# A two-layer mixture-of-experts kernel: expert weights split during layer 0, their halves kept in DRAM, and GpSimd's routed work given to VectorE

## What is computed

```
x = x + ffn0(cond0(x))      # cond: a 64x64 matrix per sequence, gathered by index
x = x + ffn1(cond1(x))      # cond1 adds a bias column as well (the "side" input)

ffn0: one 512->2048->512 network with gelu, run twice per token (top 2 of 8 routes),
      each time with the low-rank additions of its route; weighted sum of both
ffn1: shared expert 512->704->512 over all tokens
      + routed experts: top 2 of 8, each silu(x Wg) * (x Wu) -> Wd, 512->352->512
```

## Time and profile before

| | us |
|---|---|
| runs shown | 1054.9, 1051.52 and 2602.53; median 1054.9 |
| the profiled execution | 1050.06 |
| its span, first to last instruction | 1048.2 |
| PE busy in the span | 1010.6 |
| DVE, ACT, POOL busy | 524.3, 314.4, 354.5 |
| TensorE's granted clock, mean | 0.993 of full |

### The profile page before, as it was taken

How to read it: one execution, slowest core, us unless ns; L and a number is a source line. 1 busy time by engine, 2 the same in 40 slices (tenths; PEclk the granted TensorE clock), 3 DMA queues, 4 the chain that set the end, 5 groups by cost and what they waited for, 6 DMA issues and landing times.

```text
span 1048.2 us, 14852 instructions
## 1 busy us (share of the span) xinstructions
PE 1010.6 (96%) x4893; PEld 837.2 (80%) x4895; DVE 524.3 (50%) x886; ACT 314.4 (30%) x550; POOL 354.5 (34%) x351
## 2 busy tenths in 40 slices
PE   8899999999999999999999999999989999999993
PEld 5678887888888887888867777778778999999992
DVE  3788777455565455555566333665543314443000
ACT  3743332211121112111242010301144545454541
POOL 4123245410000000000042000022168889898873
PEclk9999999999999999999999999999999999999997
DMA  7387543443433434453444101005155665665433
GB/s 239 130 297 272 161 136 122 166 161 114 140 123 121 153 128 161 142 181 123 138 159 151 41 1 41 1 1 198 58 187 108 163 163 142 141 146 119 80 61 40
DMA packets 51322, 136.41 MB, mean 130 GB/s; under 512 B 8708, under 2 KB 10004, under 8 KB 50772
## 3 DMA queue, kind: packets, MB, share of 16 engines
q1 hardware_dynamic: 36660, 108.15, 30.1%
q0 software_dynamic: 12432, 25.71, 12.4%
q10 hardware_dynamic: 2192, 2.08, 0.7%
HBM read 96.85 MB, written 39.07 MB: 130 GB/s over the span
## 4 chain that ended last, share of the span: by engine, by line
PE 85%; DVE 4%; POOL 4%; DMA 2%; issue 1%; ACT 1%; ACTq 1%; PEldq 0%; POOLq 0%; PEld 0%; DVEq 0%
PE ps_y L1687 6%; PE ps_y L1689 6%; PE ps_y L1688 5%; PE ps_h L1645 5%; PE ps_h L1647 5%; PE ps_h L1646 5%; PE ps_u L1700 3%; PE ps_u L1699 3%; PE ps_h L1933 2%; PE ps_y L1933 2%; PE ps_y L1928 2%; PE ps_y L1929 2%; PE ps_y L1856 2%; PE ps_y L1857 2%; PE ps_h L1840 2%; PE ps_h L1841 2%
## 5 line engine op out<-in xcount | busy, mean ns | idle before, releaser
L1202 DVE TENSOR_TENSOR h<-h,wb 128x512 f32<-128x512 f32 x64 | 44.4, 693 | 162.6 <-ACT h L903 162.5
L897 ACT ACTIVATE h<-ps_h,bias 128x512 f32<-128x512 f32 x64 | 44.0, 689 | 235.1 <-PE ps_h L1654 235.1
L685 POOL DMA_DIRECT2D s_raw<-in_sgu x8 | 4.3, 544 | 299.9 <-DVE g_lo L1210 192.1
L1687 PE MATMUL ps_y<-w_hi,g_hi 128*128 (+1 forms) x256 | 102.2, 399 | 3.5 <-DVE g_lo L1210 3.5
L1689 PE MATMUL ps_y<-w_hi,g_lo 128*128 (+1 forms) x256 | 101.2, 395 | 0.0
L1688 PE MATMUL ps_y<-w_lo,g_hi 128*128 (+1 forms) x256 | 101.0, 395 | 0.0
L1645 PE MATMUL ps_h<-xt_hi,w_hl 128*128 128x512 f32 x256 | 100.0, 391 | 0.7 <-ACT lg_t L846 0.7
L1647 PE MATMUL ps_h<-xt_hi,w_hl 128*128 128x512 f32 x256 | 100.3, 392 | 0.0
L1646 PE MATMUL ps_h<-xt_lo,w_hl 128*128 128x512 f32 x256 | 100.2, 391 | 0.0
L1477 DVE CAST eg_hi<-e_raw 128x704 fp32r<-128x704 f32 x32 | 16.7, 581 | 138.0 <-PE ps_y L1958 125.3
L903 ACT ACTIVATE h<-ps_h,bias 128x512 f32<-128x512 f32 x64 | 43.9, 688 | 115.4 <-PE ps_h L1667 115.4
(11 more groups left out here) (319 smaller groups left out, 2455.5 us busy)
## 6 DMA issues: line engine op xcount, KB each, us to landing
w_hl<-w1s_d SPq DMA_DIRECT2D x49, 704.0 KB, 4.1
w1s_d<-w_hl SPq DMA_DIRECT2D x16, 704.0 KB, 5.9
e_raw<-in_wgu SPq DMA_DIRECT2D x8, 1408.0 KB, 7.1
w_raw<-in_w1b SPq DMA_DIRECT2D x16, 608.0 KB, 4.7
xres<-in_x SPq DMA_DIRECT2D x16, 256.0 KB, 4.5
acc<-x_d SPq DMA_DIRECT2D x4, 1024.0 KB, 7.6
xc_d<-xc SPq DMA_DIRECT2D x4, 1024.0 KB, 4.8
e_raw<-in_wdn SPq DMA_DIRECT2D x8, 512.0 KB, 8.4
```

What stands on the lines that cost most here:

```text
L1202: tt(h1[u][:], h1[u][:], wb[:, v, :], ALU.mult).then_inc(gch, 1)
L1687: mm(ps_y[:, j, :], g_hi[u][:, cols], sl(w2_hi), start=first, **kw)
```

## The change

1. **Units in layer 0.** The weights of experts 1 to 7 come in a new input `we1`, 6 units of 128 x 768 for each, 42 units `k`. In layer 0, step 16 + k, for k from 0 to 41: GpSimd loads the unit to `pre_raw` (two buffers), ScalarE copies it to `pre_hi` (`high_unit`), VectorE subtracts in place (`low_unit`), and GpSimd stores both halves in DRAM, `e_d`. The load of unit k+1 is issued behind the two stores of unit k.
2. **The routed part loads halves.** `split_expert` stays for expert 0 alone. For experts 1 to 7 SyncE loads the four parts of the two halves from `e_d` (4.46 MB an expert), for expert 1 when the last shared gate/up product is done, for the others when the last tile of the expert two before is done.
3. **GpSimd's elementwise work goes to VectorE**, which reads PSUM directly; ScalarE's three copies `xg_f`, `ru`, `rgt_f` are dropped. GpSimd is left with gathers and scatters: `gather(t + 5)`, `scatter_add(t)`, where it was `scatter_add(t - 1)` behind the elementwise work.
4. **First tile earlier.** Gathers 0 and 1 go out when the slot lists are ready; `turn_x(0)` stands behind the first of the last four shared down products.
5. The bias column is packed into `cond1`; its 32 own loads are dropped, and the other 32 go into stage 0's loop over `low_w1`.

The core of the diff:

```diff
+            pool.wait_ge(w1_lo_done, 2 + FT)
+            pool.wait_ge(w2_lo_done, FT)
+            pool.wait_ge(z_ok, 4)
+            def load_unit(k):
+                u = k % 2
+                if k >= 2:
+                    pool.wait_ge(pre_st[u], 32 * (k // 2))
+                at = k % UNITS * UW
+                pool.dma_start(pre_raw[u], we1[k // UNITS, :, at:at + UW]).then_inc(pre_in[u], 16)
+            def store_unit(k):
+                u = k % 2
+                pool.wait_ge(pre_lo_done, k + 1)
+                at = k % UNITS * UW
+                for n, src in enumerate((pre_hi[u].bitcast(F32), pre_raw[u])):
+                    pool.dma_start(e_d[k // UNITS, n, :, at:at + UW], src).then_inc(pre_st[u], 16)
+            load_unit(0)
+            load_unit(1)
+            for k in range(AHEAD):
+                store_unit(k)
+                if 1 <= k < AHEAD - 1:
+                    load_unit(k + 1)
...
             for t in range(SLOT_TILES):
-                g_low(t)
-                if t + 1 < SLOT_TILES:
-                    products(t + 1)
-                if t + 2 < SLOT_TILES:
-                    x_low(t + 2)
                 if t + 5 < SLOT_TILES:
                     gather(t + 5)
-                if t:
-                    scatter_add(t - 1)
-            scatter_add(SLOT_TILES - 1)
+                scatter_add(t)
...
+            def high_unit(k):
+                act.wait_ge(pre_in[k % 2], 16 * (k // 2 + 1))
+                nc.scalar.copy(pre_hi[k % 2], pre_raw[k % 2]).then_inc(pre_hi_done, 1)
...
                     gelus(s * FT + f, f, f % 2, s - 1 if f == 1 else None)
+                    if (s - 1) * FT + f < AHEAD:
+                        high_unit((s - 1) * FT + f)
                     if s + 1 < NS and f == 1:
                         masks(s + 1)
...
+            def low_unit(k, u):
+                dve.wait_ge(pre_hi_done, k + 1)
+                tt(pre_raw[u].bitcast(F32R), pre_raw[u], pre_hi[u].bitcast(F32), ALU.subtract).then_inc(pre_lo_done, 1)
...
                     hidden_tile(s * FT, v, 0, sums=s - 1)
+                    low_unit((s - 1) * FT, 0)
                     add_moved(s - 1)
                     hidden_tile(s * FT + 1, v, 1)
+                    low_unit((s - 1) * FT + 1, 1)
...
+            def load_halves(e):
+                b, gu = e % 2, DC * 2 * H1
+                for k, (eg, ed) in enumerate(((eg_hi, ed_hi), (eg_lo, ed_lo))):
+                    sp.dma_start(eg[:, b].rearrange("p c n -> p (c n)").bitcast(F32),
+                                 e_d[e - 1, k, :, 0:gu]).then_inc(half_in, 16)
+                    sp.dma_start(ed[:, b].rearrange("p c n -> p (c n)").bitcast(F32),
+                                 e_d[e - 1, k, :, gu:gu + HC * D]).then_inc(half_in, 16)
...
+                    if (s, j) == (NS - 1, 0):
+                        turn_x(0, 0, 16, first=True)
```

More of the change, by code:

```diff
@@ L96, in adaln_ffn @@
                              for u in range(2)])
+        ahead = ExitStack()
+        sb_ahead = tensors(ahead)
+        pre_hi = [sb_ahead(f"pre_hi{u}", [P, UW], F32R)[:] for u in range(2)]
+        pre_raw = [sb_ahead("pre_raw0", [P, UW])[:], u1t[:, 0:UW]]
+        ahead.close()
         w_raw = [sb(f"w_raw{u}", [P, WROW]) for u in range(2)]
@@ L339, in adaln_ffn @@
         out_st = sem("out_st")
+        pre_in = [sem(f"pre_in{u}") for u in range(2)]
+        pre_hi_done = sem("pre_hi_done")
+        pre_lo_done = sem("pre_lo_done")
+        pre_st = [sem(f"pre_st{u}") for u in range(2)]
+        half_in = sem("half_in")
         e_in = sem("e_in")
@@ L953, in _ @@
             for h in range(2):
[L954 removed]
+                act.wait_ge(cw1_in[h], 16 * J)
             take_x(2)
@@ L997, in _, with x_high @@
                         rows_step(*rows_step_after_down(s, j))
-            def x_high(t, first=False):
+            def x_high(t):
                 act.wait_ge(xgt_done, t + 1)
                 nc.scalar.copy(xg_hi[:].rearrange("p c n -> p (c n)"), ps_u[:, 0, :]).then_inc(xg_hi_done, 1)
-                if not first:
-                    act.wait_ge(xg_lo_done, t)
-                nc.scalar.copy(xg_f[:], ps_u[:, 0, :]).then_inc(xg_f_done, 1)
             def silu(t, u, first=False):
@@ L1036, in copies @@
                     silu(t + 1, 1 - u)
-                g_high(t, first=stored is None and n == 0)
-                if nxt:
-                    up(t + 1, 1 - u)
+                g_high(t)
                 if nxt2:
@@ L1231, in low_s @@
                     dve.wait_ge(z_done, 2 + STEPS)
+                else:
+                    for u in range(2):
+                        dve.wait_ge(pre_st[u], 32 * (AHEAD // 2))
                 hi, lo, raw = shared_halves(n)
@@ L1869, in slot_sums, with turn_x @@
                 last.then_inc(oh_mm, 1)
+            def turn_x(t, u, n, first=False):
+                pe.wait_ge(xg_in[u], n)
+                if not first:
+                    pe.wait_ge(xg_lo_done, t)
+                for c in range(DC):
+                    last = nc.tensor.transpose(ps_u[:, 0, c * P:(c + 1) * P], xg[u][:, c * P:(c + 1) * P], ident[:])
+                last.then_inc(xgt_done, 1)
             cond_rows(2)
@@ L1906, in experts @@
                 return [(packed // E ** n % E, packed // E ** n % 2) for n in range(WINDOW)]
-            def turn_x(t, u, n, first=False):
-                pe.wait_ge(xg_in[u], n)
-                if not first:
-                    pe.wait_ge(xg_f_done, t)
-                for c in range(DC):
-                    last = nc.tensor.transpose(ps_u[:, 0, c * P:(c + 1) * P], xg[u][:, c * P:(c + 1) * P], ident[:])
-                last.then_inc(xgt_done, 1)
             def gate_or_up(t, u, eb, k):
@@ L1973, in _ @@
             pe.wait_ge(rg_zero, 1)
-            turn_x(0, 0, 16, first=True)
             e = experts(0)
```

149 lines of the change are left out of this document (77 added, 72 removed).

## The result

| | before | after |
|---|---|---|
| median | 1053.8 us | 1071.4 us |
| lowest to highest | 1051.5 to 1054.9, and one of 2602.5 | 1068.0 to 1074.1 |
| ratio after to before | | 1.017, 95% interval 1.013 to 1.022 |
| span of the profiled execution | 1048.2 | 1068.0 |
| TensorE's granted clock, mean | 0.993 | 0.983 |

What follows compares the result with a forecast made beforehand. TensorE was taken as the bound, busy 1010.6 of 1048.2 us. 1050.06 less 15.2 routed gains, plus 11.3 at stage starts and 9.9 steady growth, gave 1056.1; own range 1046 to 1073, 8-in-10 range 1036 to 1084.

Steps and rivals of the forecast that it cites:

- The stall at stage 2: Start of stage 2, layer 0: TensorE waits 8.3 us for a mask copy queued behind `high_unit(17)`, plus 1.7 for the clock.
- G: Layer 0: landing time of a unit's load, counted from the first store's issue; 4.8 to 5.4 us, taken as 4.8.
- the ring: Layer 0: a unit's cycle of copy, subtraction, issue and transfers, 2.2 + G = 7.0 us, just under the 7.39 step.
- The steady growth: Stages 1 and 3: overlap with `w_hl` adds between nothing and 1.9 us to G; half taken, 18 steps of 0.55, 9.9.
- The 1.0 for `gelu_first(50)`: Start of stage 3: `high_unit(33)` holds `gelu_first(50)` on ScalarE, so `second` comes 1.0 us late.
- (c): Routed part's tail: with `scatter_add(t)` the last scatter starts 2.2 us behind the last `yt` instead of 6.8, winning 4.6.
- (a): Routed part's head: 1.5 us won before the first gate, and 3.7 between `turn_g(0)` and `turn_g(1)`.
- (b): Routed part, tiles 1 to 37: 248.0 us falls to 36 tiles of 6.74, winning 5.4.
- A: Layer 0: the units are hidden after all, load 17 in time and the ring holding; 1036 us, chance 0.13.
- B: Layer 0: the ring outlasts the step in every stage, deciding at G above 5.2; 1115 us, chance 0.12.
- C: Routed part: its gain is given back by late scatters or a tile waiting for halves; 1066 us, chance 0.10.
- D: Layer 0: VectorE holds GpSimd's issues, 0.7 us in each of 33 steps; 1079 us, chance 0.06.

Runs made afterwards that it cites:

- the kernels with 254.0: Kernels where `turn_g(0)` to `turn_g(38)` took 254.0 us, among them the changed kernel with layer 0's units left out: median 1035.5 us, ratio 0.985.
- the last kernel with the units moved: Changed kernel with load before stores, no unit in the first two steps of stages 2 and 3, `s_raw` loads not between last units: 1044.7 us, ratio 0.992.
- masks first: Changed kernel with `masks(s+1)` ahead of `high_unit` on ScalarE at a stage's second step: median 1062.4 us, ratio 1.011.
- the pieces: Changed kernel with SyncE's 1 MB transfers in layer 0 each split in four of 256 KB, one a step: median 1062.9 us, ratio 1.012.

## Why the prediction was right, and where it was not

**The stall at stage 2: right.** Predicted: 8.3 us in L1699 behind load 17, and 1.7 for the clock. Measured: 8.04 us in the same instruction, by the same chain of three lists; `hidden(34)` is 10.7 late, so the rest is 2.7. The spell at 0.50 of the clock was 6.8 us long, not 3.4. That 8.04 is so near to 8.3 has luck in it: the load landed 0.5 us later behind the first store than I put it, and `low_unit(16)` ended 0.6 us sooner against the time at which L1750 was due (308.24 against 307.17, where I had 301.1 against 299.4).

**G: the wrong end taken.** Of 4.8 and 5.4 I took 4.8, since the first transfer is a store. It was 5.3 to 5.4 (5.3 above), the value that two loads of the trace gave. So the ring was 7.5 us instead of 7.0 and a little above a step from the start: the units of stage 1 were stored 7.56 us apart (204.74 to 250.09, six of them). TensorE lost little by it: outside the gaps the steps grew by 1.4 us in all in stage 1 and 1.2 in stage 2.

**The steady growth: wrong, and with it the sum.** I put 9.9 us as 18 steps of 0.55, from the overlap with `w_hl`. Steps 0.55 longer hardly exist. In their place came four gaps, 20 us together, that no term of mine holds. The step that failed is the one that looked at one step of the trace and took `w_hl` as all that SyncE sends. At the second step of a stage it also sends 1 MB, in stage 3 another two times 1 MB. And the bound "all of 1.9" for a meeting was too low, as the run with a quarter of the bytes shows: there a load took 4.3 us more than by the median. One gap of the four, 6.1 us at `hidden(56)`, also has GpSimd's pause of 2.6 us in it; no run is without the pause, so its share is not known. The 1.0 for `gelu_first(50)` was 0.1, but the gap was waiting one step on.

**The routed gains: right in sum, two of four for another reason.** Predicted 15.2, measured 16.1. Head 1.5 and 1.5; first tile 3.7 and 3.8; tail 4.6 and 4.2. The steady part was 5.4 and 6.7 in the profiled run of after, 5.1 in the kernels with 254.0. But (c) said that the tail is won by `scatter_add(t)`: with the order put back it stays won, so it is GpSimd's freedom that wins it. Of (a), about half, 0.7, hangs on the earlier `turn_x(0)` and gathers. And (b) counted the move of the elementwise work as a gain of 5.4. That is not how it is to be priced: with the bytes of the halves in the routed part it avoids a loss of 35. What made the 0.15 us a tile in before is open, since giving the work back brought the other loss with it.

**The rivals.** A and B are out: stage 2 did stall, and its steps did not grow by 2. B's condition (G above 5.2) was met, though; what it gave was too much, for it added `w_hl` in every step. C did not occur, for the reason given against it, three tiles of cover: scatters took up to 10.7 us to land, and TensorE's longest wait in the tiles was 1.0. D is out as a mechanism: GpSimd's issues stood at 0.54 us, with two pauses. They stand at fixed counts of transfers and not at fixed work of VectorE: the smaller, at 430.6 in after, falls beside its sums, but in the last kernel with the units moved, where it ends at 444.0, beside nothing at all. The rule of the Trainium skill, "SBUF — State Buffer", "SBUF: two separate sides", that VectorE's fast copies keep GpSimd from writing descriptors, is not what the longest pause shows, for in the kernel with the load ahead VectorE is idle in half of it.

**The range** held since the case's own top end, 1073, was reached by adding 1.5 us to each of 18 steps. The amount was about right for the wrong shape.

## What to carry to other kernels

When new transfers go beside old ones, list all that the other queues send in the whole stretch, with bytes and issue times, and not only what one step shows: a transfer issued just behind a larger one of another queue may wait for all of it and for what is queued behind. Issue a load as soon as its buffer allows, ahead of the stores of the unit before; that one line (ratio 1.017 to 1.003) was worth more here than masks first (1.011) or the pieces (1.012) alone. Read the medians beside the traces: the executions of one kernel differed here by up to 17 us, and a trace shows only one. And when an engine's work is moved, ask what it would have waited for in its old place beside the new traffic; the move may be what makes the rest of the change possible.

## What was not expected of the hardware

- GpSimd transfers of 96 KB, issued within 0.5 us of a SyncE transfer of 704 KB, moved nothing for 2.8 us. Of two stores of 384 KB issued 0.8 and 0.3 us ahead of one (the kernel with the load ahead, at 302.62 and 303.15 against 303.44) the first landed in 2.7 us, as usual, and the second shared the engines with it; the queues in the stretch 305.3:307.3:

```profile
q1 hardware_dynamic: 52, 0.29, 58.7%
q0 software_dynamic: 45, 0.24, 37.3%
```

- A load of 96 KB landed in 2.3 us by the median and 6.6 at most, one of 384 KB in 4.3 and 9.1.
- GpSimd paused for 2.6 us between two issues, between the same two transfers by count in eleven kernels, and for 0.7 us or more between another two; no cause is shown.
- The distance between tiles was 6.71 us throughout in the profiled execution of after, and 6.71 and 6.79 by turns in ten other kernels whose code in that loop is the same or nearly so.
